# Both halves of the depth of each aggregation in seven products instead of one half

## The reference, cut to what matters

```python
state = x                                     # x: 2048 x 256
for _ in range(5):
    s_in  = state @ in_W.T + in_b
    s_out = state @ out_W.T + out_b
    a = concat([A @ s_in, A.T @ s_out, state])          # A: 2048 x 2048, symmetric 0/1
    r = sigmoid(a @ r_W.T + r_b)
    z = sigmoid(a @ z_W.T + z_b)
    h = tanh(concat([a_in, a_out, r * state]) @ h_W.T + h_b)
    state = (1 - z) * state + z * h
out = tanh(state @ o1_W.T + o1_b) @ o2_W.T + o2_b
return layernorm(x + out)
```

## Time and profile before

| | us |
|---|---|
| median of 3 runs | 661.27 (660.89 to 661.61) |
| the profiled execution's own time | 660.54 |
| its span, first to last instruction | 658.7 |
| TensorE busy in it | 647.0 (98%), 2908 matmuls |
| VectorE busy | 481.5 (73%) |
| ScalarE busy | 407.1 (62%) |
| GpSimd busy | 51.1 (8%) |
| TensorE in matmuls of the seven products (L646), 256 + 192 of them | 65.1 + 46.7 |
| TensorE in plain aggregation matmuls (L593), 768 of them | 178.6 |

### The profile page before, as it was taken

One profiled execution on the slowest core, in us unless ns is written; L12 is line 12 of the kernel. 1 busy time (PEld: TensorE's weight loads), 2 busy tenths in 40 slices (PEclk: granted clock), 3 DMA queues, 4 the chain that ended last, 5 costly groups with the idle time before them and its releaser, 6 DMA issues.

```text
span 658.7 us, 8626 instructions
## 1 busy us (share of the span) xinstructions
PE 647.0 (98%) x2908; PEld 535.6 (81%) x2908; DVE 481.5 (73%) x782; ACT 407.1 (62%) x544; POOL 51.1 (8%) x49
## 2 busy tenths in 40 slices
PE   8999999999999999999999999999999999999994
PEld 7888888787888888888888888888888888888884
DVE  4986988897487569838784994677489658725887
ACT  2765554479457747855593788368368935763646
POOL 0191126100400000000000000000000000000002
PEclk9999999999999999999999999999999999999998
DMA  8998757222000221300013031000312200013003
GB/s 289 354 354 218 183 193 170 35 52 46 0 1 33 57 40 36 52 8 0 32 39 57 0 68 28 0 32 32 54 43 64 33 1 0 2 65 127 1 0 132
DMA packets 106803, 48.30 MB, mean 73 GB/s; under 512 B 88976, under 2 KB 95248, under 8 KB 106512
## 3 DMA queue, kind: packets, MB, share of 16 engines
q1 hardware_dynamic: 98256, 46.82, 25.9%
q10 hardware_dynamic: 8512, 1.05, 1.1%
HBM read 33.69 MB, written 11.53 MB: 69 GB/s over the span
## 4 chain that ended last, share of the span: by engine, by line
PE 95%; DVE 3%; issue 1%; ACT 0%; POOL 0%; DVEq 0%; POOLq 0%
PE bank L593 26%; PE bank L580 17%; PE bank L582 17%; PE bank L581 17%; PE bank L646 16%; PE bank L742 2%; PE bank L771 1%; DVE stats L1629 1%; DVE a L1622 0%; DVE deg_sum L1251 0%; DVE ring L1184 0%; PE bank L818 0%; ACT a L1168 0%; DVE work L1662 0%; DVE stateT L1228 0%
## 5 line engine op out<-in xcount | busy, mean ns | idle before, releaser
L593 PE MATMUL bank<-ring,rows 128*128 128x512 f32 x768 | 178.6, 389 | 0.0
L941 ACT ACTIVATE work<-work,bias 128x512 f32<-128x512 f32 x120 | 85.9, 722 | 149.1 <-DVE work L1349 148.5
L593 PEld LDWEIGHTS bank<-ring,rows 128*128 128x128 f32 x768 | 144.1, 188 | 30.1 <-issue 0.2
L1349 DVE SCALAR_TENSOR_TENSOR work<-degree,deg_w,bank 128x512 f32<-128x512 uint16 x120 | 88.6, 745 | 54.7 <-PE bank L582 53.9
L841 ACT ACTIVATE ring<-a 128x1024 fp32r<-128x1024 uint8 (+1 forms) x115 | 116.3, 1048 | 8.8 <-PE bank L593 6.6
L580 PE MATMUL bank<-u_c,fold 128*128 128x512 f32 x240 | 93.5, 390 | 0.0
L582 PE MATMUL bank<-u_c,fold 128*128 128x512 f32 x240 | 93.4, 389 | 0.0
L581 PE MATMUL bank<-u_c,fold 128*128 128x512 f32 x240 | 93.4, 389 | 0.0
L646 PE MATMUL bank<-ring,rows 128*128 128x512 f32 x256 | 65.1, 391 | 0.0
L580 PE MATMUL bank<-st_c,own 128*128 128x512 f32 x160 | 62.4, 390 | 0.3 <-DVE st_c L1184 0.3
L581 PE MATMUL bank<-st_c,own 128*128 128x512 f32 x160 | 62.3, 389 | 0.0
(11 more groups left out here) (150 smaller groups left out, 921.5 us busy)
## 6 DMA issues: line engine op xcount, KB each, us to landing
stage<-in_adj_dram SPq DMA_DIRECT2D x15, 512.0 KB, 8.3
sums<-in_adj_dram SPq DMA_DIRECT2D x13, 512.0 KB, 5.9
turned_dram<-work SPq DMA_DIRECT2D x12, 512.0 KB, 2.6
rows<-turned_dram SPq DMA_DIRECT2D x192, 32.0 KB, 2.0
work<-in_x_dram SPq DMA_DIRECT2D x4, 512.0 KB, 10.6
x_dram<-work SPq DMA_DIRECT2D x4, 512.0 KB, 10.1
a<-x_dram SPq DMA_DIRECT2D x4, 512.0 KB, 5.3
a<-in_adj_dram SPq DMA_DIRECT2D x3, 512.0 KB, 11.0
```

What stands on the lines that cost most here:

```text
L593: m = nc.tensor.matmul(u_bank[2 * (c % 2) + d][:, :], rows[:, part, j, d * P:(d + 1) * P], tile[:, jj, :], start=(first and jj == 0 and pa ...
L941: nc.scalar.activation(gates[:, g, e, :], gates[:, g, e, :], ACT.Tanh if g == H else ACT.Sigmoid, bias=bias[:, g, e:e + 1]).then_inc(gate_ ...
L1349: nc.vector.scalar_tensor_tensor(out=gates[:, g, e, :], in0=degree[:, c * CW:(c + 1) * CW], scalar=deg_w[:, g, e:e + 1], in1=g_bank[s % 3] ...
```

## The change

Both halves of the depth now go through the seven products. `ORDER` has 28 items of 4 matmuls, 112 a side in place of 120, and nothing is left of the plain items. The banks add up over both halves, P4 gets a bank of its own (`t_bank`), and `mix` has five sums in place of six, with copies of the P1 and P5 banks made by ScalarE (`copy_p1`, `copy_p5`). VectorE casts 10 items of a side (P5 four times, as a sum of two byte tiles; the second halves of P2, P4 and P7 by a copy or a one-source sum), ScalarE 18. The second half needs row sums too (`l_add`, four on VectorE) and seven roundings in place of four; three of these go into `u_c` and `rs_c` and so are kept in DRAM for side 1 (`keep_late`, `load_late`). The matrix sums of a side for both halves fill `sums`, so those of the two sides are swapped through DRAM (`load_sums`, `store_sums`), and GpSimd makes four sets of them in place of two. The own parts of the first three gate tiles are multiplied between items 7 and 8 of the pair (`own_ahead`), for which the state of that chunk is rounded one gate chunk earlier.

```diff
-    ORDER = [(P1, 0), (P1, 1), (P6, 0), (P6, 1), (P7, 0), (P7, 1), (P2, 0), (P2, 1), (P4, 0), (P4, 1), (P5, 0), (P5, 1),
-             (1, 4), (P3, 0), (0, 4), (P3, 1), (0, 5), (1, 5), (0, 6), (0, 7), (1, 6), (1, 7)]
+    ORDER = [(P1, 0), (P1, 1), (P6, 0), (P6, 1), (P7, 0), (P7, 1), (P4, 0), (P4, 1), (P1, 2), (P1, 3), (P5, 0), (P5, 1),
+             (P5, 2), (P5, 3), (P2, 0), (P2, 1), (P3, 0), (P3, 1), (P6, 2), (P6, 3), (P2, 2), (P2, 3), (P3, 2), (P3, 3),
+             (P7, 2), (P7, 3), (P4, 2), (P4, 3)]
     NI = len(ORDER)
-    BY_ACT = [n for n, (kind, _) in enumerate(ORDER) if kind != P5]
-    BY_VECTOR = [n for n in range(NI) if n not in BY_ACT]
-    V, U3, W5, C12, C21, C22 = range(1, 7)
+    OWN_AT = ORDER.index((P1, 2))
+    OWN_AHEAD = 3
+    BY_VECTOR = [n for n, (kind, p) in enumerate(ORDER) if kind == P5 or kind in (P2, P4, P7) and p >= 2]
+    BY_ACT = [n for n in range(NI) if n not in BY_VECTOR]
+    V, C12, U3, C22, C21 = range(1, 6)
+    MIXES = 5
...
+    L11, L1, L2, L21, L22, L3, L4 = (f"l{n}" for n in ("11", "1", "2", "21", "22", "3", "4"))
+    ROWS = [(T1, 0), (T2, 0), ("b11", 0), (1, 0), (1, 1), (T3, 0), (T4, 0),
+            (L11, 0), (L1, 0), (L2, 0), (L21, 0), (L22, 0), (L3, 0), (L4, 0)]
     ADDED = [T1, T2, T4, T3]
+    ADDED_LATE = [L1, L2, L4, L3]
...
# SyncE
+            def keep_late(t):
+
+                sp.wait_ge(row_lo, row_count(t, (L2, 0)))
+                sp.dma_start(l2_dram, u_c[:, :, 0, :].bitcast(F32)).then_inc(l2_kept, 16)
+                sp.wait_ge(row_lo, row_count(t, (L4, 0)))
+                sp.dma_start(l34_dram, rs_c[:, :, :, :].bitcast(F32).rearrange("p s k w -> p (s k w)")).then_inc(l34_kept, 16)
+
+            def load_late(t):
+
+                sp.wait_ge(l2_kept, 16 * t)
+                sp.wait_ge(u_used, t * NC + 2)
+                sp.dma_start(u_c[:, :, 0, :].bitcast(F32), l2_dram).then_inc(late_back, 16)
+                sp.wait_ge(l34_kept, 16 * t)
+                sp.wait_ge(gate_done, t * S_GATE + 2 * GATE)
+                sp.dma_start(rs_c[:, :, :, :].bitcast(F32).rearrange("p s k w -> p (s k w)"), l34_dram).then_inc(late_back, 16)
+
+            def load_sums(t, side):
+
+                sp.wait_ge(pair_used, used(t, side) - NI + ORDER.index((P7, 3)) + 1)
+                sp.wait_ge(sums_kept, 64)
+                for h in range(2):
+                    sp.dma_start(sums[:, 1 - h].rearrange("p k w -> p (k w)"), sums_dram[side, h]).then_inc(sums_ready[h], 16)
...
             for t in range(1, LAST):
+                keep_late(t)
+                if t > 1:
+                    load_sums(t, 1)
                 turn_store(t, 0)
+                load_late(t)
+                if t == 1:
+                    store_sums(1)
                 turn_store(t, 1)
                 for k in range(2):
                     turn_load(t, k)
+                load_sums(t + 1, 0)
...
# TensorE, aggregate_pair
+                    if n == OWN_AT:
+                        own_ahead(t, 2 * side)
...
+                    if side == 1 and (kind, p) == (P6, 2):
+                        pe.wait_ge(late_back, 32 * t)
+                    if (kind, p) == (P2, 0):
+                        pe.wait_ge(copied, groups(t, side, 2, 1))
+                    if (kind, p) == (P3, 0):
+                        pe.wait_ge(copied, groups(t, side, 2, 2))
+            def own_ahead(t, c):
+
+                pe.wait_ge(st_lo, t * S_TWO + (c + 1) * TWO)
+                for s in range(OWN_AHEAD):
+                    wait(pe, gate_read, t * S_GATE + c * GATE + s - 2)
+                    own_part(g_bank[s % 3], s // DB, s % DB, st_c)
...
# TensorE, gate_chunk
-                    wait(pe, gate_read, t * S_GATE + c * GATE + s - 2)
-                    own_part(g_bank[s % 3], g, e, st_c)
+                    if first or c % 2 or s >= OWN_AHEAD:
+                        wait(pe, gate_read, t * S_GATE + c * GATE + s - 2)
+                        own_part(g_bank[s % 3], g, e, st_c)
...
# ScalarE
             def copy_p1(t, side):
 
-                act.wait_ge(pair_used, used(t, side) + ORDER.index((P1, 1)) + 1)
+                act.wait_ge(pair_used, used(t, side) + ORDER.index((P1, 3)) + 1)
                 if side == 0:
                     act.wait_ge(row_lo, row_count(t, (T4, 0)))
                 else:
-                    act.wait_ge(u_lo, t * S_TWO + TWO)
-                nc.scalar.activation(temp[0], u_bank[0][:, :], ACT.Copy).then_inc(p1_copied, 1)
+                    act.wait_ge(mixed, groups(t, 1, MIXES, 0))
+                nc.scalar.activation(temp[0], u_bank[0][:, :], ACT.Copy).then_inc(copied, 1)
+
+            def copy_p5(t, side):
+
+                act.wait_ge(pair_used, used(t, side) + ORDER.index((P5, 3)) + 1)
+
+                act.wait_ge(state_new, t * S_TWO + side * 2 * TWO)
+                nc.scalar.activation(tmp[:, 1, :], u_bank[1][:, :], ACT.Copy).then_inc(copied, 1)
+
+            def keep_l11(t):
+
+                act.wait_ge(rows_loaded[2], 16 * NQ * NQ * t)
+                act.wait_ge(rs_ready, t * S_TWO)
+                nc.scalar.activation(spare[1].rearrange("p (b d) -> p b d", b=BC), rows[:, LO, 2 * BC:3 * BC, 0:P].bitcast(F32), ACT.Copy)\
+                  .then_inc(l11_kept, 1)
...
# ScalarE, gate_chunk_two
                 gate(t, c, 3)
+                if not ending:
+                    for e in range(DB):
+                        split_state(*((t, 2) if c == 1 else (t + 1, 0)), e)
                 next_cast()
                 gate(t, c, 4)
                 gate(t, c, 5)
...
# ScalarE, aggregate_pair
-                cast(t, side, 4)
+                for k in range(4, 8):
+                    cast(t, side, k)
+                if side == 0:
+                    keep_l11(t)
+                    row_high(t, L11, 0)
+                cast(t, side, 8)
+                if side == 0:
+                    turn_move(t - 1, range(2))
+                cast(t, side, 9)
+                if side == 0:
+                    turn_move(t - 1, range(2, 4))
+                    row_high(t, L1, 0)
                 copy_p1(t, side)
-                for k in range(5, 10):
+                for k in range(10, 14):
                     cast(t, side, k)
-                for k in range(10, 12):
-                    if side == 0:
-                        row_high(t, 2, k - 10)
-                        turn_move(t - 1, range(2 * (k - 10), 2 * (k - 9)))
-                    cast(t, side, k)
-                for k in range(12, 16):
-                    cast(t, side, k)
-                    if k % 2 == 1:
-                        split_state(t, 2 * side, k // 2 - 6)
-                for k in range(16, 20):
-                    if side == 0 and k < 18:
-                        row_high(t, 3, k - 16)
+                copy_p5(t, side)
+                if side == 0:
+                    row_high(t, L2, 0)
+                cast(t, side, 14)
+                if side == 0:
+                    row_high(t, L21, 0)
+                cast(t, side, 15)
+                if side == 0:
+                    for k in (L22, L3, L4):
+                        row_high(t, k, 0)
+                for k in range(16, len(BY_ACT)):
...
# VectorE, cast
+                h = p // 2
+                if kind == P5:
+                    a, b = (a8[:, 2 * side + 1, (2 * h + k) * BC + 2 * (p % 2):(2 * h + k) * BC + 2 * (p % 2) + 2, :] for k in range(2))
+                    nc.vector.tensor_tensor(ring[:, n % RING], a, b, ALU.add).then_inc(std_cast, 1)
+                elif kind == P7:
+                    dve.wait_ge(sums_ready[h], sums_loads(t, side))
+                    nc.vector.tensor_scalar(ring[:, n % RING].rearrange("p j w -> p (j w)"), sums[:, 1 - h, 1, p % 2 * 2 * CW:(p % 2 + 1) * 2 * CW],
+                                            -1.0, 0.0, ALU.add, ALU.add).then_inc(std_cast, 1)
+                else:
+                    c, b = {P2: (2 * side, BC), P4: (2 * side + 1, BC)}[kind]
+                    b += 2 * BC * h + 2 * (p % 2)
+                    nc.vector.tensor_copy(ring[:, n % RING], a8[:, c, b:b + 2, :]).then_inc(std_cast, 1)
...
# VectorE, mix and l_add
+                b, a, product, last = {V: (low_, low_, u_bank[2], (P6, 3)), C12: (c12, low_, u_bank[1], (P3, 3)),
+                                       U3: (high_, low_, u_bank[3], (P7, 3)), C22: (c22, high_, p5, (P5, 3)),
+                                       C21: (c21, high_, t_bank, (P4, 3))}[what]
+            def l_add(t, k):
+
+                n = (t - 1) * 4 + ADDED_LATE.index(k)
+                raw = lambda q, d: rows[:, LO, q * BC:(q + 1) * BC, d * P:(d + 1) * P].bitcast(F32)
+                one, eleven, two = (s.rearrange("p (b d) -> p b d", b=BC) for s in spare)
+                if k == L1:
+                    dve.wait_ge(rows_loaded[2], 16 * NQ * NQ * t)
+                    dve.wait_ge(rs_ready, t * S_TWO)
                 else:
-                    dve.wait_ge(mixed, groups(t, side, 6, what - 1))
```

(81 more changed lines are left out.)

189 lines of the change are left out of this document (119 added, 70 removed).

## The result

The changed kernel takes 669.42 us (median of 4 runs, 668.31 to 670.33) against 661.09 before: a ratio of 1.0124, 95% interval 1.0107 to 1.0142. It is slower by 8 us; the forecast was 656.6. The profiled execution took 669.64, 9.1 more than the one before.

The account below looks back on a forecast made before the run. TensorE, busy 98%, was taken as the bound: 14.5 us for 64 fewer matmuls, less 9.8 of new waits (3.6 + 1.6 + 1.0 + 3.6), leaves 4.7. That gave 655.8 us profiled, 656.6 for the median, range 648 to 665.

Parts of the forecast that it names:

- GpSimd's two added sets are hidden in steps 0 and 1, where it idles: Among the edits priced at nothing: GpSimd's added matrix sums cost no time.
- d: Chunk 2, steps 1 to 3: VectorE's queue rounds chunk 3's state 1.2 us late for TensorE; 3.6 us.
- land at 37, VectorE wants them at 38: cover of 1: SyncE's row loads begin 4 us later in the pair yet land 1 us before VectorE needs them; priced at nothing.
- rival of a late transfer: Stores and loads sharing SyncE's queue delay chunk 2 and side 0; 5.0 us lost, 661.6, no change; 11%.
- beat of 0.2267 us: TensorE within a run: each matmul less saves 0.2267 us if other engines still deliver ahead.
- 64 matmuls: TensorE: 8 matmuls fewer on each of 8 sides, 14.5 us saved.
- price of a one-source instruction from bytes: VectorE's casts from bytes to `ring`, the one unknown price: taken as 0.69 us, half rate.
- rival of dear casts: VectorE's one-source casts take 1.20 us, so late items on both sides cost 14.8 us; 671.4; 13%.
- a: Every side: ScalarE's copy of the P5 bank comes 0.45 us late for P3 at item 16; 3.6 us.
- b: Side 0: roundings before item 20 in ScalarE's queue make item 19 0.4 us late; 1.6 us.
- c: Late last gate before side 0: casts of items 4 to 7 reach TensorE up to 0.25 us late; 1.0 us.
- All hidden: Rival: ScalarE and VectorE half a microsecond ahead of the count, earlier waits vanish, chunk 2's halves; 648.6; 14%.

Follow-up runs that it names:

- x1: Changed kernel with three of GpSimd's sets of matrix sums made on 4 words of each row in place of 512; 661.74 us, ratio 1.0002.
- x12: x11 with GpSimd's three added sets of matrix sums made on 4 words of each row only; 656.66 us, ratio 0.9933.
- b1: Kernel before, with only GpSimd's second set of sums (side 1) moved earlier, into chunk 2 of step 0; 665.0 us, ratio 1.0066.
- x2: Changed kernel, complete, with the same GpSimd sums spread to other times; 671.32 us, ratio 1.0158.
- x3: Changed kernel with the loads of row group 0 let go after item 11 of side 1, not item 17; 667.11 us, ratio 1.0083.
- x4: Changed kernel with chunk 3's state and aggregation rounded before the sums and roundings of the next rows on VectorE in chunk 2; 674.27 us, ratio 1.0194.
- x6: Changed kernel with no own parts between the pair's halves (OWN_AHEAD = 0); 671.76 us, ratio 1.0144.
- x9: Changed kernel with the last two of chunk 2's four row sums (T4, T3) behind gate 5 on VectorE; 668.67 us, ratio 1.0113.
- x11: x10 plus the second cast of P6 on VectorE in place of ScalarE, VectorE's other casts moved up; 664.56 us, ratio 1.005.
- x10: Changed kernel with the edits of x3, x5 and x9 together; 664.3 us, ratio 1.005.
- x5: Changed kernel with the copy of the P5 bank one cast earlier on ScalarE; 668.06 us, ratio 1.0094.

## Why the prediction was wrong

**The step that failed** is the sentence "GpSimd's two added sets are hidden in steps 0 and 1, where it idles". It looked at GpSimd's idle time only and asked nothing about who pays. Three sets fell beside VectorE's work (side 0's second half, and both halves of side 1), at 8.1 us (x1) and 7.7 (x12). No rival held it. b1 shows that the effect needs nothing of the change, and the rule of the Trainium skill cited with x2 would have been a reason to make it a rival. The trace of before had a price as well. In step 0 a VectorE sum of two tensors in on-chip memory began while GpSimd made one of its sums (VectorE's row, then GpSimd's):

```profile
100.17 1.36 DVE L1372 TENSOR_TENSOR work<-work,stateT 128x512 f32<-128x512 f32 x1
```

```profile
99.94 1.04 POOL L539 TENSOR_TENSOR sums<-a,byte_two 128x512 uint32<-128x512 uint32 x1
```

The 37 instructions of this line with no GpSimd work beside them take 0.68 or 0.69. It was one row, 0.67 us too long, and it cost TensorE nothing there. The order of the work mattered: in the kernel before, the second set stood where it cost nothing.

**The term that was mis-sized** is d, in step 1: 1.2 forecast, 4.9 measured. "land at 37, VectorE wants them at 38: cover of 1" took the end of SyncE's row for the landing, and the data come about 1.6 us later. So there was no cover in any step: VectorE waited 0.50 in step 2 and 0.34 in step 3. In step 1 the loads took 17.38 us in place of the 15.64 of the earlier trace rows, which is from step 2; the wait for the rows grew to 2.22 and TensorE's to 3.1, and this also brought 1.6 us of half clock. x3 shows the load as the cause: with it earlier d is 1.2 in each of the three steps by the table's measure, as forecast for VectorE's queue alone. Why the load is slower in step 1 is not shown, but it is no effect of the change: the kernel before has 17.23 there, a row that the prediction could have read. The rival of a late transfer had this mechanism, at 1.0 in each step.

**What held.** The beat of 0.2267 us and the 64 matmuls; the price of a one-source instruction from bytes (0.69 forecast; 0.689 and 0.690), so the rival of dear casts is refuted although its 671.4 lies near the result; a, b, c and d in steps 2 and 3 (8.6 forecast, 9.4 measured; 0.5 of the difference is VectorE's wait for the rows in d). All hidden is refuted by a alone. A wait of 0.8 us in chunk 2 of the last step and 0.3 of small ones were not foreseen. 655.8 + 0.8 (a to d) + 8.0 + 3.7 for d in step 1 + 0.8 + 0.3 = 669.4, beside 669.64.

**Expectations on experiments** failed where they took a wait away without asking what it had covered (x4, x6, x9), or took it that GpSimd's sums would cost little at another time (x2).

## What to carry to other kernels

An idle engine isn't free: before work is put on GpSimd, look at what VectorE does in the same stretch, and count each of its instructions with two inputs in on-chip memory as waiting for one of GpSimd's. A trace in which the two already overlap shows the price, if one looks for the instructions of a line that are longer than the others. Where one wait is removed on an engine that has hardly a pause in the stretch, name the wait behind it first; x4, x9 and x11 gave back most or all of theirs. Price the transfers of each step apart, from that step's rows, and count the time from the last issue to its data: here the first step's load took 1.6 us longer in the trace of before already, and the cover of 1 us was never there.

## What the runs showed that was not expected

- GpSimd is slowed as well: the same sum of 512 words a row took 1.04 to 1.30 us alone and up to 2.15 beside VectorE (x2). The trace of before has one such row too, 1.73 at 171.91 beside a VectorE rounding.
- TensorE's clock fell to 1.2 GHz around waits in stretches that were otherwise full, from 1 us before to 1.5 after TensorE went on: 1.75 us (x6, at 170.46), 2.0 (x4, at 260.15), 2.3 (x9, at 259.60) and more, up to 3.2 (x1, at 251.80). It did not at waits of 1.6 us (x10, at 131.16), 1.75 (x6, at 199.83) and 2.2 (x2, at 205.79), and a wait of 2.7 us at 132 had it in x3, x6 and b1 but not in the changed kernel or x5. So the length of the wait alone doesn't decide it. Where it fell, it cost up to 1.6 us more than the wait itself, in x1 2.8.
